# A gated cross-attention and routed feed-forward kernel: mask rows picked in SBUF, one array for the small inputs, another order of constants and first loads

## The chip, the cores and the metric

The kernel runs on 1 core of one Trainium2 chip. The metric is the device time of one execution in microseconds (us), the median of several runs. A profile of one execution shows when each engine worked: TensorE (PE, with its weight loads PEld), VectorE (DVE), ScalarE (ACT), GpSimd (POOL) and SyncE (SP), whose queue issues most of the DMAs.

## The reference

```python
def _L0_xattn_ref(hidden_states, memory_tokens, memory_mask):      # 32 x 112 x 512, 32 x 375 x 512, 32 x 375
    scores = jnp.einsum('bsd,bmd->bsm', hidden_states, memory_tokens) * scale
    scores = jnp.where(memory_mask[:, None, :], scores, neg_inf)
    attn = jax.nn.softmax(scores, axis=-1)
    readout = jnp.einsum('bsm,bmd->bsd', attn, memory_tokens)
    valid_b = jnp.any(memory_mask, axis=-1)
    return jnp.where(valid_b[:, None, None], readout, jnp.zeros_like(readout))

def _L0_ffn_ref(x, Wg, W, b):                                      # Wg 512 x 8, W 8 x 512 x 512
    probs = jax.nn.softmax(jnp.einsum('bsh,he->bse', x, Wg), axis=-1)
    combine = jax.nn.one_hot(jnp.argmax(probs, axis=-1), E) * probs
    y = jnp.einsum('bsh,ehd->bsed', x, W) + b
    return jnp.einsum('bsed,bse->bsd', y, combine)

x = x + jnp.tanh(g_xattn[0]) * _L0_xattn_ref(_layernorm(x), ctx_2048, mask_BxS2_bk0)
x = x + jnp.tanh(g_ffn[0]) * _L0_ffn_ref(_layernorm(x), L0_ffn_Wg, L0_ffn_W, L0_ffn_b)
```

All arithmetic is in 32-bit floats.

## The kernel before

The kernel has two phases. In the first, one batch (112 rows of x, its context of 375 rows) after the other goes through cross-attention and through the choice of one of 8 experts for each row; in the second, tiles of 128 rows, gathered by expert, go through the expert's weights. The change is in the first phase, and mostly ahead of its first batch.

For a batch, TensorE turns the context (four chunks of 128 columns, three transposes each, `ctx_turn`) and the normalised x (`x_turn`, four transposes); ScalarE copies each turned chunk from PSUM (`ctx_part`), VectorE computes the rest that this rounding left (`low_part`); then come the score products (`scores`; eleven, the last of which adds the row of the mask). Softmax follows on VectorE and ScalarE, its weights are turned, and `read_out` multiplies them with the context. Normalisation takes `stats1` on VectorE, a few small steps on POOL (`stats1` there) and `apply1` on ScalarE. The stages of three batches overlap: the iteration `batch(i)` on TensorE scores batch i+1, reads out batch i and turns batch i+2. It runs from i = -2 up; four iterations stand before a loop over four batches a turn. Every engine executes its own list in order and waits on semaphores.

SP's queue issues the loads. There are four buffers for x and context; `load(i+4)` is issued when `x2` of batch i, the rows with attention added, is complete, right after those rows' store to DRAM. `load_w` brings a 128 x 512 part of the expert weights for each batch, which ScalarE and POOL split into two parts (`w_hi`, `w_lo`).

Ahead of the first batch: POOL sets the constants; SP loads the mask, the router weights `wg_sb`, batch 0, the two gate scalars (each spread over 128 partitions), and batch 1; VectorE makes an additive mask of 32 rows, which SP stores to DRAM (`mask_rows`) and loads back one row per batch (`mask_row`, in partition 0 of a cleared tile). TensorE first makes `valid_ps` (which batches have a valid token), waits for `gv_ok` (that, times the gate's tanh), then sums the router weights over their rows in four products (`wg_sum_ps`), from which VectorE subtracts the mean and makes seven copies (`wg_ok`); only then does `batch(-2)` begin:

```python
            pe.wait_ge(wg_ld, 16)
            pe.wait_ge(gv_ok, 1)
            for k in range(KC):
                last = pe.matmul(wg_sum_ps, ones[:, :], wg_sb[:, k, :], start=(k == 0), stop=(k == KC - 1))
            last.then_inc(wg_mm, 1)
            pe.wait_ge(wg_ok, 7)
            for n in range(-2, 0):
                batch(Count(n))
```

Of the kernel before, what the change touches and what calls it, by code (L numbers as in the profile page):

```python
# [27 lines left out]
P = 128  # L28
# [79 lines left out]
def build(nc, x, ctx, mask, g_attn, g_ffn, w_gate, w_exp, b_exp, out):  # L108
    B, S, D = x.shape
    M = ctx.shape[1]  # L110
    E = w_gate.shape[1]
# [25 lines left out]
    FILL = 64  # L137
    assert M == MC * MP and MP <= P and KC * S + E <= 512 and REGION >= N + P and B % TURN == 0 and S < P
# [4 lines left out]
    mask_rows = nc.dram_tensor("mask_rows", (B, M), BF16, kind="Internal").ap()  # L143
    lst = nc.dram_tensor("token_list", (LIST, 4), F32, kind="Internal").ap()

    with ExitStack() as stack:
# [17 lines left out]
        first_only = sb("first_only", [P, P], BF16)  # L164
# [14 lines left out]
        mask_add = late[0:B, D + 128:D + 384].bitcast(BF16)[:, 0:M]  # L179
        wg_sb = sb("wg_sb", [P, KC, E])  # L180
        wg_mid = sb("wg_mid", [P, KC, E])
        mask_row = sb("mask_row", [P, 4, M], BF16)
        any_valid = sb("any_valid", [B, 1])
        any_diag = sb("any_diag", [B, B])
        gate_in = sb("gate_in", [P, 2])
# [81 lines left out]
        valid_ps = small_ps[:, 256:256 + B]  # L267
# [9 lines left out]
        gate_ld, wg_ld, b_ld, mask_ld = sem("gate_ld"), sem("wg_ld"), sem("b_ld"), sem("mask_ld")  # L277
# [4 lines left out]
        mask_in = [sem(f"mask_in{i}") for i in range(4)]  # L282

        fill_st, zero_st, mask_mv = sem("fill_st"), sem("zero_st"), sem("mask_mv")
# [8 lines left out]
        row_clear, first_ok = sem("row_clear"), sem("first_ok")  # L293
# [14 lines left out]
        wg_mm, wg_ok = sem("wg_mm"), sem("wg_ok")  # L308
# [13 lines left out]
        CONSTS = 16  # L322
# [41 lines left out]
        def _(sp):  # L364
# [6 lines left out]
            def load_mask(j):  # L371
                sp.dma_start(mask_row[0:1, j.slot(4), :], mask_rows[bass.ds(j.times(1), 1), :]
                             ).then_inc(mask_in[j.slot(4)], 16)

# [16 lines left out]
            load_w(Count(0))  # L391
            load(Count(2))
            load(Count(3))
            load_w(Count(1))
# [9 lines left out]
            def batch(i):  # L404
# [50 lines left out]
        def _(pool):  # L455
            pool.memset(ident[:, :], 0.0).then_inc(const, 1)
            pool.memset(ones_bf[:, :], 1.0).then_inc(const, 1)
            pool.memset(ones[:, :], 1.0).then_inc(const, 1)
            if ME > M:
# [4 lines left out]
            pool.memset(half[:, :], -0.5).then_inc(const, 1)  # L464
            pool.memset(eps[:, :], EPS).then_inc(const, 1)
            pool.memset(minus[:, :], -1.0).then_inc(const, 1)
            pool.wait_ge(const, 6)
# [835 lines left out]
```

## Time and profile before

| | |
|---|---|
| median of 3 runs | 397.51 us (397.43 to 399.56) |
| profiled execution | 396.76 us, its span 394.9 us |
| TensorE busy | 355.5 us (90%) |
| VectorE, POOL, ScalarE busy | 301.6 (76%), 227.8 (58%), 221.3 us (56%) |
| granted TensorE clock, mean | 0.982 |
| DMA | 67.26 MB, mean 170 GB/s |

The span runs from the first to the last instruction of the profiled execution; the rest of its time lies around it. Busy shares are means over the whole span, and the start, the batches and the tiles have different limits.

### The profile page before, as it was taken

What the parts mean: (1) busy time and instruction counts of PE and PEld (TensorE: products, weight loads), DVE (VectorE), ACT (ScalarE), POOL (GpSimd) and SP (SyncE); (2) the same over time, 40 slices, a digit from 0 to 9 for tenths busy, and PEclk for the clock granted to TensorE, in tenths of its full rate; (3) what the DMA queues carried; (4) which work ended last, traced back from release to release, by engine and by line L of the source; (5) the groups of instructions that cost most, each with busy time, mean ns of one, the idle gap of its engine ahead of it and who ended that gap; (6) DMA issues with size and microseconds to landing.
All of it is one profiled execution on the core that took longest, in us unless ns stands there. A gap on an engine that the chain in (4) does not pass through costs nothing.

```text
span 394.9 us, 9724 instructions
## 1 busy us (share of the span) xinstructions
PE 355.5 (90%) x2012; PEld 299.0 (76%) x2013; DVE 301.6 (76%) x1085; ACT 221.3 (56%) x488; POOL 227.8 (58%) x483
## 2 busy tenths in 40 slices
PE   0889999999999999999999999756999999999980
PEld 0668888788888878888888877635877787878860
DVE  2467989889999889989998889736887677776760
ACT  1267777667777767777776768323444444444410
POOL 6023666566666666666656655565655566666620
PEclk9999999999999999999999999979999999999996
DMA  6586788878889979889888874193445544445410
GB/s 171 146 204 170 185 212 193 194 187 221 201 200 226 188 174 237 191 184 231 209 210 185 202 190 124 42 320 85 125 148 158 162 144 142 132 149 159 152 56 0
DMA packets 40222, 67.26 MB, mean 170 GB/s; under 512 B 11298, under 2 KB 11878, under 8 KB 40200
## 3 DMA queue, kind: packets, MB, share of 16 engines
q1 hardware_dynamic: 33576, 50.43, 52.2%
q0 software_dynamic: 6624, 16.58, 13.3%
q8 instruction: 8, 0.13, 0.2%
q14 instruction: 14, 0.11, 0.1%
HBM read 51.70 MB, written 17.12 MB: 174 GB/s over the span
## 4 chain that ended last, share of the span: by engine, by line
PE 54%; DMA 14%; DVE 10%; issue 8%; POOL 5%; SPq 4%; ACT 2%; POOLq 1%; DVEq 1%; ACTq 0%
PE read_both L1143 8%; PE ctx_ps L1087 8%; PE read_both L1144 7%; DMA ctx_sb<-in_ctx 6%; PE score_ps L1184 4%; PE score_ps L1182 4%; PE score_ps L1183 3%; PE score_ps L1112 3%; POOL out_rows L603 3%; DMA li<-token_list 3%; PE score_ps L1109 3%; PE score_ps L1110 3%; DMA x_sb<-mid_rows,take 3%; PE score_ps L1111 3%; PE prob_ps L1096 2%
## 5 line engine op out<-in xcount | busy, mean ns | idle before, releaser
L1143 PE MATMUL read_both<-ctx_sb 125*112 125x264 f32 x192 | 61.1, 400 | 2.1 <-DVE lg L841 1.8
L1182 PE MATMUL score_ps<-w_hi,ctxT_hi 128*128 x140 | 58.8, 420 | 1.6 <-DVE ctxT_lo L912 1.6
L972 DVE TENSOR_TENSOR ctxT_lo<-ctx_ps,ctxT_hi 128x375 fp32r<-128x375 f32 x96 | 49.5, 542 | 13.9 <-ACT ctxT_hi L641 13.5
L530 POOL DMA_INDIRECT token_list<-pay,pos x32 | 32.6, 1018 | 47.0 <-DVE pos L893 41.5
L1087 PE MATMUL ctx_ps<-ident,ctx_sb 125*128 125x125 f32 x384 | 54.4, 278 | 5.9 <-DMA ctx_sb<-in_ctx 2.6
L1144 PE MATMUL read_both<-ctx_sb 125*112 125x256 f32 x192 | 57.1, 379 | 0.0
L1184 PE MATMUL score_ps<-w_lo,ctxT_hi 128*128 x140 | 55.8, 398 | 0.0
L1183 PE MATMUL score_ps<-w_hi,ctxT_lo 128*128 x140 | 55.4, 396 | 0.0
L1087 PEld LDWEIGHTS ctx_ps<-ident,ctx_sb 125*128 125x128 f32 x384 | 43.8, 145 | 8.4 <-DMA ctx_sb<-in_ctx 3.5
L594 POOL DMA_INDIRECT x_sb<-mid_rows,take x35 | 34.4, 983 | 27.0 <-DVE ctx_sb L930 13.6
L652 ACT ACTIVATE w_raw<-x_sb,li 128x512 f32<-128x512 f32 x35 | 28.5, 815 | 36.9 <-DMA x_sb<-mid_rows,take 36.9
L603 POOL DMA_INDIRECT out_rows<-ctx_sb,put x35 | 39.4, 1126 | 16.9 <-issue 9.2
L641 ACT ACTIVATE ctxT_hi<-ctx_ps 128x375 fp32r<-128x375 f32 x96 | 42.7, 482 | 8.5 <-PE ctx_ps L1087 7.6
L706 ACT ACTIVATE xn<-x_sb,ln 112x512 f32<-112x512 f32 x32 | 26.0, 813 | 30.3 <-POOL ln L494 30.3
L665 ACT ACTIVATE ctxT_hi<-ctx_ps 128x512 fp32r<-128x512 f32 x35 | 20.9, 598 | 36.0 <-PE ctx_ps L1164 36.0
L479 POOL TENSOR_TENSOR w_lo<-w_raw,w_hi 128x512 f32 (+1 forms) x32 | 40.8, 1274 | 0.0
L1144 PEld LDWEIGHTS read_both<-ctx_sb 125*112 125x112 f32 x192 | 34.0, 177 | 8.7
L1109 PE MATMUL score_ps<-ctxT_hi,xnT_hi 128*120 128x384 f32 x96 | 38.0, 396 | 0.9 <-DVE ctxT_lo L972 0.9
L925 DVE SCALAR_TENSOR_TENSOR x_sb<-ctx_sb,li,x_sb 128x512 f32<-128x512 f32 x35 | 26.4, 754 | 13.3 <-issue 12.8
L1143 PEld LDWEIGHTS read_both<-ctx_sb 125*112 125x112 f32 x192 | 29.2, 176 | 5.6 <-issue 2.2
L912 DVE TENSOR_TENSOR ctxT_lo<-ctx_ps,ctxT_hi 128x512 fp32r<-128x512 f32 x35 | 24.2, 691 | 11.6 <-ACT ctxT_hi L665 11.5
L1110 PE MATMUL score_ps<-ctxT_hi,xnT_lo 128*120 128x384 f32 x96 | 32.4, 337 | 0.0
(136 smaller groups left out, 816.0 us busy)
## 6 DMA issues: line engine op xcount, KB each, us to landing
ctx_sb<-in_ctx SPq DMA_DIRECT2D x32, 672.0 KB
w_raw<-in_L_ffn_W SPq DMA_DIRECT2D x32, 256.0 KB, 4.6
x_sb<-in_x SPq DMA_DIRECT2D x32, 224.0 KB, 4.0
mid_rows<-x SPq DMA_DIRECT2D x32, 224.0 KB, 3.1
ctx_sb<-in_ctx SPq DMA_DIRECT2D x32, 78.0 KB
ctx_sb<-in_L_ffn_b SPq DMA_DIRECT2D x8, 256.0 KB, 6.2
li<-token_list SPq DMA_DIRECT2D x35, 2.0 KB, 1.9
x_sb<-mid_rows,take POOLq DMA_INDIRECT x35, 3.4
```

The source lines that it names most:

```text
L479: pool.tensor_tensor(w_lo[:, bass.ds(w.times(D), D)], w_raw[:, w.slot(2), :], w_hi[:, bass.ds(w.times(D), D)].bitcast(F32), ALU.subtract). ...
L603: pool.indirect_dma_start(out, bass.IndirectOffsetOnAxis(put[:, b:b + 1], 0), res[:, b, :], None, bounds_check=N - 1, oob_is_err=False).th ...
L641: act.activation(ctxT_hi[:, k, 0:M], ctx_ps[k % 2][:, 0:M], ACT.Copy).then_inc(ctxT_hi_ok, 1)
L972: dve.tensor_tensor(ctxT_lo[:, k, 0:M], ctx_ps[k % 2][:, 0:M], ctxT_hi[:, k, 0:M].bitcast(F32), ALU.subtract).then_inc(ctxT_ok, 1)
L1087: last = pe.transpose(ctx_ps[k % 2][:, c * MP:(c + 1) * MP], ctx_sb[0:MP, MC * j.slot(4) + c, SE + k * P:SE + (k + 1) * P], ident[0:MP, 0:MP])
L1109: pe.matmul(score_ps[a][0:SE, 0:MG], xnT_hi[:, k, :], ctxT_hi[:, k, :], start=(k == 0), stop=False)
L1110: pe.matmul(score_ps[a][0:SE, 0:MG], xnT_lo[:, k, :], ctxT_hi[:, k, :], start=False, stop=False)
L1143: pe.matmul(read_a, turned[:, 0:S], turned[:, S:SE + HALF], start=(c == 0), stop=(c == MC - 1))
L1144: last = pe.matmul(read_b, turned[:, 0:S], turned[:, SE + HALF:], start=(c == 0), stop=(c == MC - 1))
L1182: pe.matmul(y_ps[a][:, :], hi, w_hi[:, chunk], start=(k == 0), stop=False)
L1183: pe.matmul(y_ps[a][:, :], lo, w_hi[:, chunk], start=False, stop=False)
L1184: last = pe.matmul(y_ps[a][:, :], hi, w_lo[:, chunk], start=False, stop=(k == KC - 1))
```

## The change

Mask rows: the additive mask stays in SBUF as `mask_add` (128 partitions, rows 32 and up zero). The last score product takes as its weights column j of the identity, repeated with step 0, so that row j is picked; store, loads and `mask_row` go away. Small inputs: the host lays router weights and both scalars in one array of 128 x 34, which ScalarE's queue loads, as it does the mask. Router sum: VectorE adds the four parts first, and one product is left. Constants: POOL sets those of the start first, the others (`router_constants`) after the first statistics. TensorE: 40 and 16 products of constants ahead of `batch(-2)`, and the wait for `wg_ok` now ahead of the first scores. `x_turn` of batch 0 goes ahead of chunks 2 and 3, and chunks 0 and 1 of context 1 go behind the scores of batch 0. SP waits for `st1_ok` ahead of load 1, for `xnT_ok` ahead of load 2 and for context 1 ahead of the second part of the weights.

```diff
@@ build
+    WARM, WARM_MORE = 40, 16
-        valid_ps = small_ps[:, 256:256 + B]
+        valid_ps = read_both[:, 0:B]
+        warm_ps = score_ps[1][:, 0:P]
...
@@ sync
-            sp.dma_start(mask_u8[:, :], mask).then_inc(mask_ld, 16)
-            sp.dma_start(wg_sb[:, :, :], w_gate.rearrange("(k p) e -> p k e", p=P)).then_inc(wg_ld, 16)
             load(Count(0))
-            sp.dma_start(gate_in[:, 0:1], g_attn.rearrange("(a b) -> a b", a=1).to_broadcast([P, 1])).then_inc(gate_ld, 16)
-            sp.dma_start(gate_in[:, 1:2], g_ffn.rearrange("(a b) -> a b", a=1).to_broadcast([P, 1])).then_inc(gate_ld, 16)
+            sp.wait_ge(st1_ok, 1)
             load(Count(1))
-            sp.wait_ge(mask_ok, 2)
-            sp.dma_start(mask_rows, mask_add[:, :]).then_inc(mask_mv, 16)
-            sp.wait_ge(mask_mv, 16)
-            sp.wait_ge(row_clear, 1)
-            for j in range(4):
-                load_mask(Count(j))
             load_w(Count(0))
+            sp.wait_ge(xnT_ok, 1)
             load(Count(2))
+            sp.wait_ge(ctx_ld[1], 32)
+            load_w(Count(1))
             load(Count(3))
-            load_w(Count(1))
...
                     load(i.plus(4))
-                    load_mask(i.plus(4))
@@ gpsimd
-            pool.memset(ident[:, :], 0.0).then_inc(const, 1)
             pool.memset(ones_bf[:, :], 1.0).then_inc(const, 1)
+            pool.memset(ident[:, :], 0.0).then_inc(ident_ok, 1)
+            pool.memset(mask_add[:, :], 0.0).then_inc(mask_clear, 1)
...
-            pool.memset(mask_row[:, :, :], 0.0).then_inc(row_clear, 1)
...
                 if at == -3:
-                    late_constants()
+                    router_constants()
@@ scalar
-            act.wait_ge(gate_ld, 32)
+            act.dma_start(mask_u8[:, :], mask).then_inc(mask_ld, 16)
+            act.dma_start(small_sb[:, :], small).then_inc(small_ld, 16)
+            act.wait_ge(small_ld, 16)
             act.activation(gate_th[:, :], gate_in[:, :], ACT.Tanh).then_inc(th_ok, 1)
...
+                    if at == -1:
+                        weights(ahead)
+                        act.wait_ge(w_ld[0], 16)
                     act.activation(w_hi[:, bass.ds(ahead.times(D), D)], w_raw[:, ahead.slot(2), :], ACT.Copy
                                    ).then_inc(w_hi_ok, 1)
-                    if at != B - 2:
+                    if at not in (-1, B - 2):
                         weights(ahead)
@@ vector
+            def sum_router():
+
+                dve.wait_ge(small_ld, 16)
+                dve.tensor_reduce(wg_part[:, :], wg_sb[:, :, :].rearrange("p k e -> p e k"), AX.X, ALU.add).then_inc(wg_part_ok, 1)
+
+            def mark_valid():
+                dve.wait_ge(ident_ok, 2)
+                dve.tensor_copy(ident_bf[:, :], ident[:, :]).then_inc(select_ok, 1)
+                dve.wait_ge(mask_ok, 2)
+                dve.tensor_scalar(any_diag[:, :], ident[0:B, 0:B], any_valid[:, :], None, ALU.mult).then_inc(any_ok, 1)
...
                 if at == -3:
+                    sum_router()
+                    mark_valid()
+                    center_router()
                     which_valid()
-                    center_router()
@@ tensor
-                pe.wait_ge(mask_in[j.slot(4)], j.rounds(4) * 16 + 16)
-                pe.matmul(score_ps[a][0:S, 0:M], first_only[:, 0:S], mask_row[:, j.slot(4), :],
+                pe.matmul(score_ps[a][0:S, 0:M], ident_bf[:, bass.ds(j.times(1), 1)].to_broadcast([P, S]), mask_add[:, :],
                           start=False, stop=True).then_inc(score_mm, 1)
...
                 if at == -1:
-
-                    ctx_turn(turned, 0)
-                    ctx_turn(turned, 1)
+                    pe.wait_ge(select_ok, 1)
+                    pe.wait_ge(mask_ok, 2)
+                    pe.wait_ge(wg_ok, 7)
...
-            pe.wait_ge(any_ok, 1)
-            pe.matmul(valid_ps, ones[0:B, :], any_diag[:, :], start=True, stop=True).then_inc(valid_mm, 1)
-            pe.wait_ge(wg_ld, 16)
-            pe.wait_ge(gv_ok, 1)
-            for k in range(KC):
-                last = pe.matmul(wg_sum_ps, ones[:, :], wg_sb[:, k, :], start=(k == 0), stop=(k == KC - 1))
-            last.then_inc(wg_mm, 1)
-            pe.wait_ge(wg_ok, 7)
...
+            pe.wait_ge(const, 1)
+            for n in range(WARM):
+                pe.matmul(warm_ps, ones_bf[:, :], ones_bf[:, :], start=True, stop=True)
+            router_sum()
+            valid_sum()
+            for n in range(WARM_MORE):
+                pe.matmul(warm_ps, ones_bf[:, :], ones_bf[:, :], start=True, stop=True)
+            pe.wait_ge(ident_ok, 2)
             for n in range(-2, 0):
                 batch(Count(n))
```

On TensorE the program began with these rows, from the valid sum (L1259) and the router sum (L1263) to the first score product of batch 0 (L1109); `ctx_ps` holds the turned context and `prob_ps` the turned x.

```order
L1259 MATMUL small_ps<-any_diag,w_lo 128x32
L1263 MATMUL small_ps<-wg_sb,w_lo 128x8 x4
L1087 MATMUL ctx_ps<-ident,ctx_sb 128x125 x12
L1096 MATMUL prob_ps<-ident,xn 128x112 x4
L1087 MATMUL ctx_ps<-ident,ctx_sb 128x125 x6
L1109 MATMUL score_ps<-ctxT_hi,xnT_hi 120x384
```

With the change the same place on TensorE reads as follows, where L1260 and L1264 are the products of constants and L1082 the transposes of the context.

```order
L1260 MATMUL score_ps<-ones_bf 128x128 x40
L1252 MATMUL small_ps<-wg_part,w_lo 128x8
L1256 MATMUL read_both<-any_diag,w_lo 128x32
L1264 MATMUL score_ps<-ones_bf 128x128 x16
L1082 MATMUL ctx_ps<-ident,ctx_sb 128x125 x6
L1091 MATMUL prob_ps<-ident,xn 128x112 x4
L1082 MATMUL ctx_ps<-ident,ctx_sb 128x125 x6
L1104 MATMUL score_ps<-ctxT_hi,xnT_hi 120x384
```

The router sum has one product and stands between the two groups of constants, x is turned in the middle of context 0, and context 1 is no longer turned ahead of the first scores.

On SP's queue the first twelve DMAs were these (L366 is a load of x, L368 and L369 of its context).

```order
L379 DMA w_lo<-in_mask_BxS_bk 32x375
L380 DMA wg_sb<-in_L_ffn_Wg 128x4x8
L366 DMA x_sb<-in_x 112x512
L368 DMA ctx_sb<-in_ctx 112x3x512
L369 DMA ctx_sb<-in_ctx 13x3x512
L382 DMA gate_in<-in_g_xattn 128x1
L383 DMA gate_in<-in_g_ffn 128x1
L366 DMA x_sb<-in_x 112x512
L368 DMA ctx_sb<-in_ctx 112x3x512
L369 DMA ctx_sb<-in_ctx 13x3x512
L386 DMA mask_rows<-w_lo 32x375
L372 DMA mask_row<-mask_rows 1x375 x4
```

With the change SP's queue begins with the first two loads and the first part of the weights (L373), then the third load and the second part.

```order
L366 DMA x_sb<-in_x 112x512
L368 DMA ctx_sb<-in_ctx 112x3x512
L369 DMA ctx_sb<-in_ctx 13x3x512
L366 DMA x_sb<-in_x 112x512
L368 DMA ctx_sb<-in_ctx 112x3x512
L369 DMA ctx_sb<-in_ctx 13x3x512
L373 DMA w_raw<-in_L_ffn_W 128x512
L366 DMA x_sb<-in_x 112x512
L368 DMA ctx_sb<-in_ctx 112x3x512
L369 DMA ctx_sb<-in_ctx 13x3x512
L373 DMA w_raw<-in_L_ffn_W 128x512
```

Mask, router weights and scalars have left the queue, and load 0 stands first.

## Rows read from the trace of the kernel before

**Rows 1.** The page's span in 40 slices: TensorE busy, granted clock, in tenths.

```profile
PE   0889999999999999999999999756999999999980
PEclk9999999999999999999999999979999999999996
```

**Rows 2.** Timeline of TensorE at the start: start, us, operation, count, idle before and releaser.

```profile
10.24 1.85 PE L1263 MATMUL small_ps<-wg_sb,w_lo 128*128 128x8 f32 x8 [3.84 <-DVE gv L797]
13.13 1.51 PE L1087 MATMUL ctx_ps<-ident,ctx_sb 125*128 125x125 f32 x6 [1.05 <-DVE ctxT_full L814]
...
18.74 0.40 PE L1109 MATMUL score_ps<-ctxT_hi,xnT_hi 128*120 128x384 f32 x1
...
21.02 0.32 PE L1114 MATMUL score_ps<-mask_row,first_only 128*112 128x375 bf16 x1
...
22.56 0.99 PE L1087 MATMUL ctx_ps<-ident,ctx_sb 125*128 125x125 f32 x6 [0.83 <-DVE ctxT_lo L972]
24.45 0.41 PE L1109 MATMUL score_ps<-ctxT_hi,xnT_hi 128*120 128x384 f32 x1 [0.90 <-DVE ctxT_lo L972]
...
27.22 0.81 PE L1087 MATMUL ctx_ps<-ident,ctx_sb 125*128 125x125 f32 x6
28.24 0.70 PE L1143 MATMUL read_both<-ctx_sb 125*112 125x264 f32 x2 [0.21 <-ACT ctx_sb L691]
```

**Rows 3.** Timeline of SP's queue at the start.

```profile
0.79 0.40 SPq L379 DMA_DIRECT2D w_lo<-in_mask_BxS_bk  x1
...
1.71 0.49 SPq L366 DMA_DIRECT2D x_sb<-in_x  x1
...
5.04 0.43 SPq L366 DMA_DIRECT2D x_sb<-in_x  x1
...
14.84 0.43 SPq L366 DMA_DIRECT2D x_sb<-in_x  x1
```

**Rows 4.** Timeline of POOL, VectorE and ScalarE at the start.

```profile
0.93 0.21 POOL L457 MEMSET ones_bf<- 128x128 bf16 x1
...
4.60 0.69 DVE L779 BATCH_NORM_STATS2 st<-x_sb 112x6 f32<-112x512 f32 x1 [1.24 <-DMA x_sb<-in_x]
...
6.61 0.19 POOL L494 TENSOR_TENSOR ln<-ve,ln 112x1 f32<-112x1 f32 x1
...
9.53 0.20 ACT L633 ACTIVATE gate_th<-gate_in 128x2 f32<-128x2 f32 x1 [7.46 <-DMA gate_in<-in_g_ffn]
9.64 0.80 ACT L706 ACTIVATE xn<-x_sb,ln 112x512 f32<-112x512 f32 x1
```

**Rows 5.** DMA view of 0 to 20 us: GB/s per half microsecond; an issue's landing.

```profile
GB/s 0 0 0 23 15 52 143 279 127 131 328 385 238 267 136 148 242 336 315 287 258 241 101 28 15 3 0 0 3 2 34 61 324 414 176 82 233 328 369 250
...
w_lo<-in_mask_BxS_bk SPq DMA_DIRECT2D x1, 11.7 KB, 1.6
```

**Rows 6.** The page's costliest groups: busy us, mean ns of one, idle before.

```profile
L972 DVE TENSOR_TENSOR ctxT_lo<-ctx_ps,ctxT_hi 128x375 fp32r<-128x375 f32 x96 | 49.5, 542 | 13.9 <-ACT ctxT_hi L641 13.5
...
L641 ACT ACTIVATE ctxT_hi<-ctx_ps 128x375 fp32r<-128x375 f32 x96 | 42.7, 482 | 8.5 <-PE ctx_ps L1087 7.6
```

**Rows 7.** Timeline of SP's queue in the loop: stores of finished rows, batches 0, 1, 26.

```profile
33.17 0.35 SPq L409 DMA_DIRECT2D mid_rows<-x  x1
...
40.33 0.33 SPq L409 DMA_DIRECT2D mid_rows<-x  x1
...
224.30 0.33 SPq L409 DMA_DIRECT2D mid_rows<-x  x1
```

**Rows 8.** The tile of the mask row: count, ns min/median/max, first and last start.

```profile
L372 SPq DMA_DIRECT2D mask_row<-mask_rows x32: 232/247/414, 13.3 to 235.4; - x32
L1114 PEld LDWEIGHTS score_ps<-mask_row,first_only x32: 128/130/130, 20.7 to 249.4; 128*112 128x112 bf16 x32
```

**Rows 9.** Waits (us, times, longest us): SP's queue to 60 us; TensorE, whole span.

```profile
SPq L409 <- DVE x L828: 14.3, 4, 4.5
...
PE ctx_ps L1087 <- DMA ctx_sb<-in_ctx: 2.6, 4, 0.8
```

More of the change, by code:

```diff
@@ L105, in run, with build @@
         body(Count(n))
-def build(nc, x, ctx, mask, g_attn, g_ffn, w_gate, w_exp, b_exp, out):
+def build(nc, x, ctx, mask, small, w_exp, b_exp, out):
     B, S, D = x.shape
     M = ctx.shape[1]
-    E = w_gate.shape[1]
+    E = b_exp.shape[0]
     N = B * S
@@ L462, in _ @@
                 pool.memset(ctxT_full[:, M:ME], 0.0).then_inc(pad_ok, 1)
-            pool.memset(mask_row[:, :, :], 0.0).then_inc(row_clear, 1)
[L464 to L467, printed above, removed]
-            pool.affine_select(out=ident[:, :], in_=ident[:, :], compare_op=ALU.not_equal, fill=1.0, base=0,
-                               pattern=[[-1, P]], channel_multiplier=1).then_inc(const, 1)
-            pool.affine_select(out=first_only[:, :], in_=ones_bf[:, :], compare_op=ALU.is_ge, fill=0.0, base=0,
-                               pattern=[[0, P]], channel_multiplier=-1).then_inc(first_ok, 1)
+            pool.memset(unused[:, :, :], 0.0).then_inc(fill_ok, 1)
+            pool.wait_ge(fill_ok, 1)
+            pool.memset(unused[:, :, 0:1], float(NO_TOKEN)).then_inc(fill_ok, 1)
+            pool.wait_ge(const, 5)
             filing = Stage(pool, "filing", -2)
@@ L531, in file @@
                                         pay[:, j.slot(4), :], None).then_inc(list_st[j.slot(4)], 16)
-            pool.iota(token_ids[:, :], [[S, B]], base=0, channel_multiplier=1).then_inc(const, 1)
-            pool.memset(zeros[:, :], 0.0).then_inc(zero_ok, 1)
-            pool.affine_select(out=before[:, :], in_=ones_bf[:, :], compare_op=ALU.is_gt, fill=0.0, base=0,
-                               pattern=[[1, P]], channel_multiplier=-1).then_inc(const, 1)
-            pool.iota(rev[:, :], [[-1, E]], base=E, channel_multiplier=0,
-                      allow_small_or_imprecise_dtypes=True).then_inc(const, 1)
@@ L736, in batch @@
                 if soon.within(B):
-                    if at != -2:
-                        turned_x(soon)
+                    turned_x(soon)
                     ctx_part(soon, 2)
-                if ahead.within(B):
+                if ahead.within(B) and at != -1:
                     act.wait_ge(w_ld[ahead.slot(2)], ahead.rounds(2) * 16 + 16)
@@ L1033, in batch @@
                     place(gated)
-                if soon.within(B) and at != -2:
+                if soon.within(B):
                     turned_x(soon)
-                if soon.within(B):
                     low_part(soon, 2)
@@ L1128, in ranks @@
                 a = j.slot(2)
+                if j.turn is None and j.at == 0:
+                    pe.wait_ge(const, 9)
                 pe.wait_ge(hot_ok, j.times(1, 1))
@@ L1140, in read_out @@
                         pe.wait_ge(lg_ok, j.times(1))
+                    else:
+                        pe.wait_ge(gv_ok, 1)
                 turned = ctx_sb[0:MP, MC * j.slot(4) + c, :]
@@ L1218, in batch @@
                     turn_weights(now)
-                if turned.within(B) and at != -1:
+                if turned.within(B):
                     ctx_turn(turned, 0)
@@ L1291 @@
     arrays, args = {}, []
+    gate_rows = _np.asarray(inputs["L0_ffn_Wg"])
+    gate_rows = gate_rows.reshape(-1, 128, gate_rows.shape[1]).transpose(1, 0, 2).reshape(128, -1)
+    scalars = [_np.broadcast_to(_np.asarray(inputs[n]).reshape(1, 1), (128, 1)) for n in ("g_xattn", "g_ffn")]
+    inputs = dict(inputs, small=_np.concatenate([gate_rows] + scalars, axis=1))
     for name in _INS:
```

108 lines of the change are left out of this document (52 added, 56 removed).

## The prediction

> **What bounds the kernel now.** The page comes first: in 40 slices TensorE is busy for nine tenths or more nearly everywhere; the first slice (9.9 us) is empty, the next two are at 8, and some near the middle and the end are lower [rows 1]. The change works on the start. TensorE's timeline there [rows 2] shows the router sum at 10.24, the first transpose of context 0 at 13.13, the first score product of batch 0 at 18.74, that of batch 1 at 24.45, and the first read-out product at 28.24. From the fourth slice on TensorE is full.
>
> What holds the 13.13? The rows of the other engines [rows 4] give the chain backwards: transposes behind the last router copy on VectorE (the releaser in the row of 13.13), those copies behind the router sum on TensorE (10.24, 1.85 us), that behind gv on VectorE (its releaser), that behind the tanh on ScalarE at 9.53, which had sat idle for 7.46 us for the two gate scalars. These stand on SP's queue behind x 0 and context 0. The layer norm of batch 0 was ready far earlier (its last POOL step at 6.61), but stands behind the tanh on ScalarE (9.64).
>
> Context 0 was not what was waited for. In the flow of bytes [rows 5] the slices of 0.5 us sum to 994 kB at 7.0 us and 1062 kB at 7.5; by their shapes mask (12 kB), router weights (16), x 0 (229) and context 0 (768) are 1025 kB, so if the queue serves in order context 0 was in at about 7.2 us. Some 6 us lie between that and the first transpose.
>
> After the start a batch takes 7.16 us at first (SP stores x2 at 33.17 and 40.33), and 7.35 on the mean up to 224.30 (26 batches) [rows 7]. Each batch's stored rows release the load four batches on, so the loop runs by its own distances: a start that is earlier by so much should move everything behind it by as much.
>
> **The change, part by part.** The profiled execution took 396.76 us (span 394.9, 1.86 around it); the median shown is 397.51, 0.75 more. Removed work in the loop first: the mask row's load, 0.25 us of SP's issuing per batch [rows 8]. No row waits for it, and SP itself waits for x2 (14.3 us in four waits at the start [rows 9]). I price it at 0. Bounds: 0, and 32 times 0.25 = 8 us of gain if SP's queue were the bound, which its waits exclude. The product that adds the mask has the same size; only its weights now come from one column of the identity with step 0. The nearest weight load is 0.13 us [rows 8], under a longer fp32 product: 0 again, with a rival below.
>
> Start of the transposes, T0. Two things must be there.
> - Context 0. x 0 goes out at 0.79, SP's first slot, in place of 1.71 [rows 3], so everything of context 0 moves 0.92 earlier: 6.3 us. Mask and gates now go on ScalarE's queue at that time; the mask landed 1.6 us after its issue [rows 5], the other array (17 kB) is as small, and their cover is the 3 us before x 0 is in. If they are mixed with context 0 instead, it costs a few tenths.
> - TensorE. The 40 + 16 products of 128 columns begin when ones_bf is set, now POOL's first instruction: 0.79 + 0.21 [rows 3, 4] = 1.0. Six transposes of 125 columns (fp32, two passes) take 1.51 us at 13.13 and 0.81 at 27.22 [rows 2], one pass about 0.105 or 0.053 us; so 40 bf16 products take 2.2 to 4.3 us and end at 3.2 to 5.3. The router sum waits for VectorE: x 0 in at 0.79 + 2.89 = 3.68 (issue 1.71, bn_stats at 4.60 [rows 3, 4]), bn_stats 0.69, two small steps of 0.2: 4.8 us. One product instead of four (1.85 / 4 = 0.46), then the valid sum, as much again, held until the identity's copy and any_diag are done (two more small steps, 5.4): 5.9. Then 16 more products, 0.9 to 1.7: TensorE is free at 6.9 to 8.1. I take 7.1, nearer the lower end since products of that row's pace were reached once TensorE had worked for 5.6 us.
>
> So T0 = 7.1 against 13.13: **-6.0 us**. The router copies now run beside the transposes (wg_ok is asked for only by the first scores): sum at about 5.5, seven small VectorE steps as between 12.09, the end of the sum before, and 13.13: done at about 6.6. Their cover is the whole transposing stage; without it they cost 1 us. x 0 normalised: the last POOL step ended at 6.80, 2.20 after bn_stats began, plus 0.8 of ScalarE [rows 4]: 3.68 + 3.0 = 6.7, before its transposes. POOL's constants that went behind it (router_constants) run while POOL has nothing else until the statistics of batch 1.
>
> T0 to the first scores took 5.6 us. With the clock up and x's transposes ahead of chunks 2 and 3 the chain is three transposes 0.5, ScalarE's copy 0.48, VectorE's rest 0.54, then transposes of chunk 2, copy and rest once more, and a hop of 0.05 at each step [rows 2, 6]: 3.4 us. ScalarE's copy of x (smaller than one of a chunk) fits before that of chunk 2. Scores at 10.5: **-2.2 us**.
>
> First scores to second took 5.71 (18.74 to 24.45). Chunks 0 and 1 of context 1, formerly turned before the scores, now come behind them: 2.65 us of scores (18.74 to 21.34, and a hop) and another 3.4 = 6.05: **+0.35 us**. Second scores at 16.55. Are context 1 and 2 there? SP issues load 1 when bn_stats of x 0 is done, 4.4 against 5.04, so it is in by about 10.7 (the bytes of the first two loads were through by 11.5 [rows 5]; needed at 13.2). Load 2 waits for xnT_ok, about 9.6, against 14.84 [rows 3], weights 0 ahead of it; behind what is still in the queue its 1 MB is in at about 15.5, and wanted at 19.4. What is queued behind that wait (weights 1, load 3, the list's fill) has some 7 us to spare.
>
> Second scores to the first read-out (3.79) keeps its chain; x 2's statistics now stand behind the softmax bias: **+0.1 us**. First read-out at 20.4 to 20.5 in place of 28.24.
>
> Sum: -6.0 - 2.2 + 0.35 + 0.1 = -7.75; 396.76 - 7.75 = 389.0, and 0.75 more on the scale of the median: **389.7 us**.
>
> **Clock.** The granted clock reads full (2.4 GHz) over the start [rows 1], yet the transposes of batch 0, to 18.7 us, run at near half the pace of those at 27.22 [rows 2]; after the first score products they were at full pace, and a stretch of transposes alone (six in 0.99 us at 22.56, a wait of 0.83 before the row) did not lose it. By the durations then the early products raise the pace and the 3.4 us of transposes keep it. The Trainium skill speaks against this ("TensorE: Matmul & The Clock Gate", Part 4: PE-mode transpose): transposes do not count as work that brings the full clock. The slow transposes of batch 0 agree with it; those at 27.22, amid other products, run fast all the same.
>
> **The rivals.**
> - The pace falls back. If T0 to the scores is transposes only and TensorE drops to the slow level, the stage keeps most of its 5.6 us and the first scores (2.6 us) run slow for about half their length: 1.8 + 1.2 us back, 392.7. For it: the slow transposes at 13.13 to 18.7 although TensorE was busy. Against: the six at 22.56. The rule just cited would act so, by this mechanism.
> - The DMA queue takes the gain back. In the loop 26 batches lost 0.19 us each against 7.16, 5 us [rows 7], and TensorE waited for contexts four times, 2.6 us [rows 9]; if the queue is the true bound, only idle time removed from it counts: the hole of 11.5 to 15.5 us [rows 5] and 0.9 at the start, some 4.9 us of gain: 392.6. For it: those losses. Against: loads are released by finished batches, so a delay is not made up by a queue that stood idle early.
> - Each load on its own: context 2 or 3 is late since it waits for xnT_ok. It needs more than 3.9 us of delay over the 15.5; each us beyond costs one. 391 to 392.
> - Slower: the weight load from one column with step 0 has no row. If each took so long that a batch's score group grew by more than 7.75 / 32 = 0.24 us, the change loses: at 0.35 the time is 401. Against: 0.13 us for the same 112 columns, with a longer product in front to hide it.
> - It does nothing: excluded unless the start is not on the path; that TensorE is full from the fourth slice on speaks against it.
>
> **How the numbers follow.** My forecast (388.0 to 391.2 by T0 from 6.4 to 8.1 and the spread of runs) has 0.58; pace 0.13; queue 0.15; late loads 0.07; slower 0.04; none or next to none 0.03. Leaving 0.1 at each end gives 386.8 to 393.2. A measurement tells 0.5%, 2 us, from no change: faster 0.92, same 0.04, slower 0.04.
>
> **What would show it.** Right: first transpose near 7, scores near 10.5 and 16.5, first read-out near 20.5, six transposes in about 0.8 us, and x2 stores that begin near 25.4 with the same spacing. Wrong: a tanh or router sum that again ends after 6 us, a first transpose behind the 16 products beyond 8 us, transposes at 1.5 us for six, TensorE waiting for a context between 12 and 30 us, or a batch longer than 7.35 on the mean.

## The result and the profile after

The changed kernel took 393.17 us (median of 4 runs, 392.07 to 394.58); the kernel before, over 4 runs, 398.53 (397.43 to 402.15): a ratio of 0.9886 (95% interval 0.9846 to 0.9926), some 4.5 us. The ratios, here and below, are of the fast runs alone and need not be the quotients of the medians beside them. Forecast were 389.7 us and a gain of 7.75. Beside the later runs, with 17 to 28 runs of the kernel before each, the same kernel gave 0.9899 (0.9863 to 0.9934) and 0.9894 (0.9859 to 0.9930). The profiled execution of the change took 394.58 us, its span 392.8.

The page's slices first (TensorE busy, granted clock, in tenths; beside [rows 1]; the clock of the first slices is no reading, as shown below), then TensorE's timeline at the start (start, us, operation; beside [rows 2]):

```profile
PE   7799999999999999999999999376999999999980
...
PEclk9999999999999999999999999968999999999995
```

```profile
1.06 4.45 PE L1260 MATMUL score_ps<-ones_bf 128*128 128x128 bf16 x40 [1.06 <-POOL ones_bf L444]
5.52 0.43 PE L1252 MATMUL small_ps<-wg_part,w_lo 128*128 128x8 f32 x2
...
6.22 1.07 PE L1264 MATMUL score_ps<-ones_bf 128*128 128x128 bf16 x16
8.18 0.83 PE L1082 MATMUL ctx_ps<-ident,ctx_sb 125*128 125x125 f32 x6 [0.89 <-DMA ctx_sb<-in_ctx]
...
11.74 0.40 PE L1104 MATMUL score_ps<-ctxT_hi,xnT_hi 128*120 128x384 f32 x1 [0.90 <-DVE ctxT_lo L968]
...
17.72 0.40 PE L1104 MATMUL score_ps<-ctxT_hi,xnT_hi 128*120 128x384 f32 x1 [0.90 <-DVE ctxT_lo L968]
...
21.57 0.70 PE L1141 MATMUL read_both<-ctx_sb 125*112 125x264 f32 x2 [0.28 <-ACT ctx_sb L680]
```

First transposes 8.18 against 13.13, first scores 11.74 against 18.74, read-out 21.57 against 28.24: the start is 6.67 us shorter. TensorE was through with its products at 7.29 (6.22 + 1.07) and then waited 0.89 for context 0. The engines ahead of it (beside [rows 4]), SP's first loads of x (beside [rows 3]) and its stores in the loop (beside [rows 7]):

```profile
0.79 0.20 POOL L444 MEMSET ones_bf<- 128x128 bf16 x1 [0.29 <-POOLq L1288]
...
3.49 0.53 DVE L758 TENSOR_SCALAR mask_add<-w_lo 32x375 bf16<-32x375 uint8 x1 [3.37 <-DMA w_lo<-in_mask_BxS_bk]
...
4.40 0.67 DVE L769 BATCH_NORM_STATS2 st<-x_sb 112x6 f32<-112x512 f32 x1
...
3.84 0.20 ACT L622 ACTIVATE gate_th<-small_sb 128x2 f32<-128x2 f32 x1 [0.82 <-DMA small_sb<-in_small]
```

```profile
0.79 0.40 SPq L366 DMA_DIRECT2D x_sb<-in_x  x1
...
5.10 0.36 SPq L366 DMA_DIRECT2D x_sb<-in_x  x1
...
10.69 0.33 SPq L366 DMA_DIRECT2D x_sb<-in_x  x1
...
26.38 0.35 SPq L398 DMA_DIRECT2D mid_rows<-x  x1
33.55 0.34 SPq L398 DMA_DIRECT2D mid_rows<-x  x1
...
216.88 0.34 SPq L398 DMA_DIRECT2D mid_rows<-x  x1
```

26 batches took 190.50 us here and 191.13 before: the loop passed the start on, 6.79 us at the first store and 7.42 at the 27th. What is lost is lost behind the loop. There the second phase begins with POOL's gather of the first tile's rows, which ScalarE then normalises (timelines of POOL and ScalarE, the kernel before and then the change):

```profile
254.92 1.00 POOL L594 DMA_INDIRECT x_sb<-mid_rows,take  x1 [0.16 <-issue]
...
260.22 0.81 ACT L652 ACTIVATE w_raw<-x_sb,li 128x512 f32<-128x512 f32 x1 [4.15 <-DMA x_sb<-mid_rows,take]
```

```profile
247.51 1.00 POOL L581 DMA_INDIRECT x_sb<-mid_rows,take  x1 [0.16 <-issue]
...
254.84 0.81 ACT L641 ACTIVATE w_raw<-x_sb,li 128x512 f32<-128x512 f32 x1 [6.46 <-DMA x_sb<-mid_rows,take]
```

The gather is issued 7.41 us earlier, its rows are used 5.38 earlier: it took 5.30 us before and takes 7.33 now. TensorE stands in this wait (waits: us, times, longest; beside [rows 9]):

```profile
PE ctx_ps L1162 <- ACT w_raw L641: 10.6, 7, 5.5
PE ctx_ps L1082 <- DMA ctx_sb<-in_ctx: 2.6, 4, 0.9
```

The waits for contexts are what they were. Before, the first of these rows read 7.1 us, 5 times, 3.2 at most.

### The profile page after: what moved, and what is told of

Read it like the earlier page. It is cut to its first block, busy times and chain, and to the rows that moved or that the text cites. A ratio compares the mean times of both kernels' runs of the same rounds, so it can differ in the third digit from the quotient of the medians.

```text
span 392.8 us, 9753 instructions
## 1 busy us (share of the span) xinstructions
PE 359.2 (91%) x2062; PEld 302.1 (77%) x2063; DVE 301.0 (77%) x1087; ACT 220.6 (56%) x488; POOL 226.8 (58%) x482
## 4 chain that ended last, share of the span: by engine, by line
PE 52%; DMA 16%; issue 9%; DVE 7%; POOL 6%; ACT 3%; SPq 3%; POOLq 1%; DVEq 1%; ACTq 0%
DMA ctx_sb<-in_ctx 8%; PE read_both L1141 8%; PE ctx_ps L1082 8%; PE read_both L1142 7%; DMA x_sb<-mid_rows,take 6%; PE score_ps L1180 4%; PE score_ps L1107 3%; POOL out_rows L590 3%; PE score_ps L1182 3%; PE score_ps L1181 3%; PE score_ps L1104 3%; PE score_ps L1105 3%; PE score_ps L1106 3%; PE prob_ps L1091 2%; PE ctx_ps L1162 2%
## 5 line engine op out<-in xcount | busy, mean ns | idle before, releaser
L1180 PE MATMUL score_ps<-w_hi,ctxT_hi 128*128 x140 | 59.7, 426 | 1.6 <-DVE ctxT_lo L908 1.6
L1082 PE MATMUL ctx_ps<-ident,ctx_sb 125*128 125x125 f32 x384 | 52.6, 272 | 4.4 <-DMA ctx_sb<-in_ctx 2.6
L1181 PE MATMUL score_ps<-w_hi,ctxT_lo 128*128 x140 | 56.3, 402 | 0.0
L1082 PEld LDWEIGHTS ctx_ps<-ident,ctx_sb 125*128 125x128 f32 x384 | 42.4, 141 | 7.0 <-DMA ctx_sb<-in_ctx 2.7
L926 DVE SCALAR_TENSOR_TENSOR ctx_sb<-score_ps,li,x_sb 128x512 f32<-128x512 f32 x35 | 26.3, 751 | 8.7 <-PE score_ps L1182 7.7
## 6 DMA issues: line engine op xcount, KB each, us to landing
w_raw<-in_L_ffn_W SPq DMA_DIRECT2D x32, 256.0 KB, 5.1
ctx_sb<-in_L_ffn_b SPq DMA_DIRECT2D x8, 256.0 KB, 7.6
```

The lines of the kernel that those rows point to most:

```text
L1082: last = pe.transpose(ctx_ps[k % 2][:, c * MP:(c + 1) * MP], ctx_sb[0:MP, MC * j.slot(4) + c, SE + k * P:SE + (k + 1) * P], ident[0:MP, 0:MP])
L1180: pe.matmul(y_ps[a][:, :], hi, w_hi[:, chunk], start=(k == 0), stop=False)
L1181: pe.matmul(y_ps[a][:, :], lo, w_hi[:, chunk], start=False, stop=False)
```

## The experiments

Times from "issue of the first gather to ScalarE's first normalised rows" are called the first gather below.

**Is the gain stable, and what are the products worth?** e1 is the change unaltered. e2 leaves out the 56 products that only occupy TensorE:

```diff
-    WARM, WARM_MORE = 40, 16
+    WARM, WARM_MORE = 0, 0
```

e3 holds load 1 back until context 0 is in:

```diff
             sp.wait_ge(st1_ok, 1)
+            sp.wait_ge(ctx_ld[0], 32)
             load(Count(1))
```

> The changed kernel unaltered, to see what of its time repeats. Theory A (the gain of the start passes on in full, and the tile phase of the profiled execution was a bad draw): stores of the last finished rows again near 252.6 us, and a tile phase after that store of about 135 us as before the change, so a span near 388 and a ratio near 0.980 to 0.984. Rival B (the tile phase is longer with the change): again some 140 us behind the last store, span near 392, ratio near 0.989.

> The 56 products of constants ahead of the first transposes are left out (their result is used nowhere). Theory A (they set the pace of the first transposes): first transpose again near 8.2 us since context 0 is waited for, six transposes in about 1.5 us in place of 0.83, first scores 1.3 to 2 us later than 11.74, first read-out near 23 to 23.5 in place of 21.57, the total 1.5 to 2 us longer. Rival B (the pace is not theirs to set, or hidden): first scores within 0.3 us of 11.74 and no difference in total.

> SP issues load 1 only when all of context 0 is in, in place of after the first statistics. Theory A (context 0 lands at 8.0 us because load 1, issued from 5.1, shares the DMA engines with it): first transpose at 6.8 to 7.2 in place of 8.18, that is what I had forecast; context 1 comes later, at 12 to 13, still in time for 14.2, so a first read-out near 20.5. Rival B (context 0 is late through its own slowest engine): first transpose at 8.0 to 8.3 still, load 1 issued at 8.1, and context 1 either just in time or waited for up to 1 us at 14.3.

Measured beside one another, 28 runs of the kernel before at 399.57 us: e1 395.78, ratio 0.9899 (0.9863 to 0.9934); e2 396.82, 0.9940 (0.9903 to 0.9978); e3 396.40, 0.9924 (0.9887 to 0.9961). TensorE's timeline in e1:

```profile
6.60 1.89 PE L1264 MATMUL score_ps<-ones_bf 128*128 128x128 bf16 x16
8.28 1.46 PE L1082 MATMUL ctx_ps<-ident,ctx_sb 125*128 125x125 f32 x6
...
12.33 0.41 PE L1104 MATMUL score_ps<-ctxT_hi,xnT_hi 128*120 128x384 f32 x1 [0.89 <-DVE ctxT_lo L968]
```

With the same 56 products as in the first profile, the 16 took 1.89 us, not 1.07, and the six transposes 1.46, not 0.83: full pace came only by the scores, 0.6 us lost. Behind its last store e1 took 139.6 us, the change's first profile 140.1: the second phase did not come out shorter. Without the products (e2) the scores too ran slow, and the read-out began at 24.02: against e1's 22.17 the products are worth 1.85 us at that place. In time e2 lies 1.0 us above e1, with intervals that overlap. In e3 the transposes began at 7.40, but context 1 then was late by 1.68 us and the read-out began at 22.69: nothing gained.

**Pacing.** e7 takes SP's three waits between its first loads out:

```diff
-            sp.wait_ge(st1_ok, 1)
             load(Count(1))
             load_w(Count(0))
-            sp.wait_ge(xnT_ok, 1)
             load(Count(2))
-            sp.wait_ge(ctx_ld[1], 32)
             load_w(Count(1))
             load(Count(3))
```

> The change with SP's three waits between its first loads taken out: load 1, weights 0, load 2, weights 1 and load 3 are issued back to back behind load 0. Theory A (loads that stand on the queue at once share the DMA engines, as load 1 did with context 0 in e3, where context 0 landed 0.8 us earlier once load 1 was held): context 0 lands at 9 to 10.5 us in place of 8.0 to 8.2, the first read-out is later by 1 to 2.5 us, and the time is 0.5 to 2.5 us above the change's. Rival (the queue serves in order, pacing is worth nothing): first transposes at 8.0 to 8.4 and the same time within 0.5 us. A third, that x 0 itself is late by sharing: bn_stats later than 5.5 us and a router sum behind it.

394.82 us, ratio 0.9907 (0.9857 to 0.9958), as the change. The transposes began at 7.59, no later. So the pacing by compute has no part that these runs can tell, and e3's earlier context 0 isn't shown to come from load 1: over the profiles of the change and its variants that leave the first loads alone, T0 lay between 7.59 and 8.85.

**The first gather and the bias loads.** Right with that gather SP issues eight loads that spread the experts' bias rows over 128 partitions (256 KB each). e4 moves them behind the landing of the first two gathers, e6 does the same to the kernel before, e5 is the kernel before unaltered:

```diff
-            sp.wait_ge(read_mm, B - 3)
-            for e in range(0, MC):
-                load_bias(e)
...
             batch(Count(B - 1))
+            sp.wait_ge(read_mm, B - 1)
+            sp.wait_ge(row_ld[0], 16)
+            sp.wait_ge(row_ld[1], 16)
+            for e in range(0, E):
+                load_bias(e)
```

> SP loads the eight expert bias rows (256 KB each, spread over the partitions) only when the first two gathers of rows have landed; it formerly issued six of them at the time of the first gather. Theory A (the first gather of the tile phase takes 7.3 us because it shares the DMA engines with the bias loads, and TensorE then waits 5.5 us and runs the next products at half pace): the first gather lands in 3 to 4 us, TensorE's wait ahead of the first tile falls to 1 to 3 us, the total falls by 2 to 4 us. Rival B (the gather is late for itself, or the biases are then what is late): the gather still takes 5 us and more, or VectorE waits for the biases at its first tile; the total is the same or 1 to 3 us longer.

> The kernel before, unaltered, for a second profile. The stretch from the last x2 store to the end took 135.2 us in its first profile and 139.5 to 140.2 in two profiles of the change. Theory A (the tile phase varies from run to run and the first profile of before was a good draw): this profile has 137 to 140 us there, a profiled time of 398.5 to 401, with the first read-out product again near 28.2. Rival (the change itself lengthens the tile phase, for instance since its first gather meets the bias loads differently): 135 to 136 us again and a time near 397. A third: the start of before is what varies; then its first read-out is more than 0.5 us off 28.2.

> The kernel before with only the eight bias loads moved behind the landing of the first two gathers (the same edit as in e4, without the change). Theory A (the meeting of bias loads and first gather is in both kernels and the change has no part in it): the first gather takes about 4.1 us to ScalarE's first normalised rows in place of 5.3 to 7.3, and the time falls by 1 to 3 us, a ratio of 0.993 to 0.9975 to before. Rival (only the change brings them together, so e4 repaired something that the change had done): ratio 0.999 to 1.001.

e4: 393.85 us, 0.9839 (0.9795 to 0.9882), some 0.6% below e1 with intervals that overlap a little, and a first gather of 4.1 us. e6: 400.90 us, 1.0124 (1.0030 to 1.0217), outside both ranges that were expected; against the median of all 23 runs of the kernel before beside it, 399.81, it is 0.3% more, so a loss isn't certain, but the gain of e4 is missing. That points to something which the change has and the kernel before hasn't. e5 took 400.67 us, with 5.73 us for the first gather, and 140.4 us behind the last store where the first profile had 135.3 and the change's 140.1: that profile of before, on which the sum was made, was a good draw in the second phase. The longer draw goes with a second fall of the clock: in the second phase the trace's clock records read 0.50 from 261.32 to 268.14 and from 274.97 to 281.80 us in e5, and only from 260.95 to 267.78 in the first profile. No run tests that by itself.

What the change has shows in the DMA view of 2 us, from 1 us behind the gather's issue: the second profile of before (254.9 to 256.9) and the change (248.5 to 250.5).

```profile
DMA packets 229, 0.44 MB, mean 219 GB/s; under 512 B 21, under 2 KB 21, under 8 KB 229
```

```profile
DMA packets 50, 0.10 MB, mean 51 GB/s; under 512 B 0, under 2 KB 0, under 8 KB 50
```

The bias loads' first packets stall: 50 of them kept the DMA engines busy for 92% of the 2 us. By the trace's packet records those of 2 KB that began in 248.5 to 249.0 took 1.33 us each (median); in the first profile of before, in 256.0 to 256.5, 0.09. The gathers' packets come behind them.

Four kernels ask what in the change does it. f1 declares the bias array first, which should shift the arrays' places in the chip's memory (no trace here shows addresses); f2 adds an unused tile that should put x_sb, ctx_sb and what follows back to their old places in SBUF; f3 brings the scratch array mask_rows back and writes it once; f4 also its 32 loads:

```diff
-_INS = ["x", "ctx_2048", "mask_BxS2_bk0", "small", "L0_ffn_W", "L0_ffn_b"]
+_INS = ["L0_ffn_b", "x", "ctx_2048", "mask_BxS2_bk0", "small", "L0_ffn_W"]
...
-    build(nc, *args, out)
+    build(nc, *args[1:], args[0], out)
```

```diff
+        pad = sb("pad", [P, 1109], BF16)
         x_sb = sb("x_sb", [P, 4, D])
```

```diff
+    mask_rows = nc.dram_tensor("mask_rows", (B, M), BF16, kind="Internal").ap()
...
+            sp.wait_ge(mask_ok, 2)
+            sp.dma_start(mask_rows, mask_add[0:B, :]).then_inc(mask_mv, 16)
+            sp.wait_ge(mask_mv, 16)
+            for j in range(4):
+                load_mask(Count(j))
...
                     load(i.plus(4))
+                    load_mask(i.plus(4))
```

> The change with the bias array declared first among the input arrays, not last (all else alike). In all five profiles of the change whose bias loads stand where they stood, the first gathered rows reach ScalarE 7.3 to 7.4 us behind the gather's issue, in the two of before 5.3 and 5.7; in the second 2 us of the bias loads the DMA engines moved 44 packets (e1) against 230 (before, second profile). Theory A (where the arrays lie in the chip's memory changed, since the change takes away and joins arrays, and the bias rows' reads now meet something there): here the stretch is another one, 5.2 to 6 us, and the bias packets flow from the start. Rival B (not the place of the bias array; its loads meet another part of the change): 7.2 to 7.5 us again.

> The change with an unused tile of 2218 bytes a partition ahead of x_sb, so that x_sb, ctx_sb and all behind them lie where they lay before in SBUF. Theory C (where ctx_sb lies in SBUF decides how the broadcast bias rows are taken): 5.2 to 6 us from the first gather's issue to ScalarE's normalised rows. Rivals A and B (memory arrays, or another part): 7.2 to 7.5 us again.

> The change with the scratch array mask_rows back between mid_rows and token_list, written once behind SP's first loads and never read. Theory A (the places of arrays in memory, here of token_list behind mask_rows): 5.2 to 6 us for the first gather. Rival (it was the loads of mask rows, or the input arrays): 7.2 to 7.5 us.

> The change with the mask rows' store and its 32 loads back on SP's queue, into a tile that nothing reads (the score product keeps the row picked in SBUF). Theory D (the loads, a row of 750 bytes each batch on SP's queue, had been keeping something ready or set the queue's order): 5.2 to 6 us for the first gather, and SP's issue some 0.25 us longer in a batch. Rival (the place in memory alone, or an input's): as in the run with the store alone. The time itself: SP's issue is hidden, so within 1 us of the change's, 393 to 396, unless the first gather changes.

Packets in the same stretch of 2 us and the first gather: f2 57 packets, 7.25 us; f3 50, 6.97; f4 15, 7.32. And f1 (247.2 to 249.2), 5.37 us:

```profile
DMA packets 250, 0.49 MB, mean 243 GB/s; under 512 B 24, under 2 KB 24, under 8 KB 250
```

Only the order of the arrays takes the stall away. Single times here were 390.66, 390.89, 393.92 and 393.95 us in the order f1 to f4, too spread to rank (f2 has the stall and is low).

**Is the stall the missing time, and what stands behind it?** All on one chip: g1 the change, g2 the bias array first, g3 that and TensorE kept busy in the wait for the first rows, g4 the kernel before with the bias array first. e8 had tried the fillers (32 and 24) with the late bias loads of e4. The edit of g3:

```diff
+            def fill(n):
+                for _ in range(n):
+                    pe.matmul(warm_ps, ones_bf[:, :], ones_bf[:, :], start=True, stop=True)
...
                 if at == B - 1:
+                    fill(56)
                     tile(Count(-1))
+                    fill(24)
```

> The change, with the bias loads behind the first two gathers as in e4, and TensorE filled where it waits for the first gathered rows: 32 products of 128 columns before the transposes of tile 0 and 24 between them and its products (their results are not used). Theory A (TensorE drops to the lower of its levels in that wait and then runs the first dozen products of the tile phase at half pace; kept busy it stays at full pace): six to twelve products of tile 0 at 0.39 us each and 0.23 apart, not 0.63 and 0.43, the time 1.5 to 3 us below that of e4, 391 to 392.5 on the scale of 397.5 before. Rival (the pace falls by TensorE's own history before the wait, not by the wait): the clock still reads 0.5 for 4 to 8 us there and the time is that of e4 within 0.5 us, or above it by what the fillers outlast the gather, up to 1.5 us.

> The change, unaltered, timed beside the next three on the same chip. By the two runs so far: a ratio of 0.988 to 0.991 to before; first gathered rows 7.3 to 7.4 us behind the gather's issue.

> The change with the bias array declared first, now timed. Theory A (the slow first packets of the bias loads, a matter of where the array lies, cost the change 1.6 to 2 us at the first gather, on the path): 1.5 to 2.5 us below the change on the same chip, a ratio to before of 0.983 to 0.986. Rival (what is lost there has slack, the list loads or the last two batches' routing set the start of the tile phase): within 0.5 us of the change.

> The bias array first, and TensorE filled with 56 products of 128 columns ahead of the transposes of tile 0 and 24 behind them (results unused). Theory (TensorE drops to half pace in the wait for the first gathered rows): products of tile 0 at 0.39 us and not 0.63, a further 1 to 2 us below the run with the bias array first alone, a ratio of 0.978 to 0.983. Rival (the time is held by the gathers and lists there, not by TensorE's pace): as the run before within 0.5 us; and if the fillers outlast the gather, up to 1 us above it.

> The kernel before with the bias array declared first. Its bias packets flowed from the start already (first gather 5.3 and 5.7 us), so by theory A nothing is to be had: ratio 0.997 to 1.003. Rival (the order of arrays helps by something else that both kernels have, such as the loads of contexts or weights): 0.99 to 0.996, and then a part of what the run with the bias array first shows is not the stall.

| kernel | median us | ratio to before (95% interval) | first gather us |
|---|---|---|---|
| before, 17 runs | 400.20 | 1 | 5.3, 5.7 |
| g1 the change | 395.64 | 0.9894 (0.9859 to 0.9930) | 7.6 |
| g2 bias array first | 393.72 | 0.9834 (0.9792 to 0.9876) | 5.4 |
| g3 and fillers | 390.52 | 0.9728 (0.9693 to 0.9764) | 6.2 |
| g4 before, bias array first | 401.47 | 1.0027 (1.0002 to 1.0051) | 5.8 |

The order of arrays is worth 1.9 us to the change and nothing to the kernel before. The intervals of g1 and g2 overlap, but the first gather agrees in every profile: 7.0 to 7.6 us in the nine with the change's order of arrays and early bias loads, 5.3 to 5.8 in the three of the kernel before (g4 among them) and 5.4 in f1 and g2; g3's 6.2 has no stall at its start. TensorE's waits agree too. Its longest for ScalarE's normalised rows, 5.5 us in the change, was 5.1 to 5.7 in those nine, 3.2 to 3.9 in those three and 3.5 and 3.6 in f1 and g2; the row of g2 reads:

```profile
PE ctx_ps L1162 <- ACT w_raw L641: 6.8, 6, 3.6
```

So the stall is on the path, and it's the change's own. The fillers gave 3.2 us more, where 1 to 2 were expected. TensorE's timeline of tile 0's products in the change, then in g3:

```profile
255.70 1.11 PE L1162 MATMUL ctx_ps<-ident,w_raw 128*128 128x128 f32 x4 [5.49 <-ACT w_raw L641]
258.39 0.79 PE L1180 MATMUL score_ps<-w_hi,ctxT_hi 128*128 x1 [1.57 <-DVE ctxT_lo L908]
258.98 0.63 PE L1181 MATMUL score_ps<-w_hi,ctxT_lo 128*128 x1
```

```profile
256.41 0.66 PE L1162 MATMUL ctx_ps<-ident,w_raw 128*128 128x128 f32 x4 [1.24 <-ACT w_raw L641]
...
258.66 0.50 PE L1180 MATMUL score_ps<-w_hi,ctxT_hi 128*128 x1 [0.25 <-DVE ctxT_lo L908]
259.00 0.39 PE L1181 MATMUL score_ps<-w_hi,ctxT_lo 128*128 x1
```

And the granted clock there (windows: sum, PE busy, clock, DMA share, GB/s) in g1, then g3:

```profile
256.00:260.00 4.00, 1.19 (x5) 0.50 1.05 399
260.00:264.00 4.00, 4.00 (x11) 0.50 0.44 117
```

```profile
256.00:260.00 4.00, 3.33 (x34) 1.00 1.05 402
260.00:264.00 4.00, 3.02 (x19) 1.00 0.33 95
```

Left idle for 5 us TensorE is granted the lower level (1.2 GHz, 0.50) and works through tile 0 at half pace; kept busy it stays at 2.4.

e8 came to 392.66 us, 0.9867 (0.9823 to 0.9911), no lower than e4's 0.9839, where 1.5 to 3 us less had been expected: the products ran at 0.39 us there too, but VectorE then waited for a list:

```profile
263.49 0.15 DVE L891 CAST take<-li 128x1 uint32<-128x1 f32 x1 [4.96 <-DMA li<-token_list]
```

The lists of the next tiles stand on SP's queue behind the eight bias loads, so loads moved late there come back as a late list: VectorE's wait at that place was 3.49 us in e4 and 2.69 in e6, and at most 1.25 in g2 and g3. In e6 this can eat what its shorter first gather (4.84 us) gives, and in e4 and e8 a part of it; another order of arrays has no such price. g3 is the best kernel of this study, faster than both.

## Why the prediction was wrong

The steps, in its order:

- **T0, 13.13 to 7.1, -6.0 us: mis-sized.** It is -4.95 (8.18). TensorE's side was nearly as worked out, free at 7.29, though by another way: the mask landed 2.7 us after its issue, not 1.6, its two VectorE steps stood in front of bn_stats (4.40, not 3.68), and the router sum came at 5.52 for 4.8. (The bounds of 6.9 to 8.1 don't follow from their terms: 5.9 and 0.9 to 1.7 make 6.8 to 7.6.) What failed is the price of context 0. "If the queue serves in order context 0 was in at about 7.2 us", less 0.92, gave 6.3. The trace's records of landings have its last part in at 9.02 us before and at 8.04 with the change: the shift is as forecast, 0.98, but the 7.2 was 1.8 us too early. The sum of bytes moved is no landing time. With load 1 issued at once (e7) context 0 was in at 7.45 and with load 1 held back (e3) at 7.27, so sharing with load 1 isn't shown to be what was missed.
- **T0 to scores, 5.6 to 3.4:** 3.56. **To the second scores, 6.05:** 5.98. **To the read-out, 3.89:** 3.85. These three terms held. The read-out came at 21.57, 1.1 us later than forecast, nearly all of it from T0.
- **Loop and mask at 0:** right. The product that adds the mask takes 0.322 us as before, and the weight load from one column with step 0 costs what the old one did:

```profile
L1108 PE MATMUL score_ps<-mask_add,ident_bf x30: 322/322/323, 20.0 to 233.7; 128*112 128x375 bf16 x30
L1108 PEld LDWEIGHTS score_ps<-mask_add,ident_bf x29: 128/130/130, 27.2 to 233.4; 128*112 x24, 128*112 128x112 bf16 x5
```

  Its rival of a loss has nothing behind it.
- **"A start that is earlier by so much should move everything behind it by as much": the step that failed.** It held through the loop and not at the first gather, where 2.0 us went (7.33 for 5.30). Nothing in the change's code touches that place; it changes which arrays lie in memory, and with their order changed once more the loss is gone (f1, g2). The prediction took the removed arrays for removed transfers alone and had no term for what they do to the second phase; by g1 and g2 that term is 1.9 us.
- **The scale.** 396.76 us, the profile that the sum was made against, and the median of 397.51 lie low: three later sets of 17 to 28 runs had medians of 399.57 to 400.20, and its second profile took 400.67. In the ratio this drops out. That 393.17 lies inside the range of 386.8 to 393.2, at its very end, is luck of the same kind: two later sets of the change had medians of 395.78 and 395.64.
- **Clock.** "The granted clock reads full (2.4 GHz) over the start" is no reading. In the trace of the kernel before the clock records begin at 18.61 us, and the page counts a stretch without a record as full, its mean of 0.982 too. The pace rose where the records begin: at 18.61 before, 5.67 in the change, 10.21 in e1, 16.07 in e2. Ahead of that TensorE worked at the lower level's pace: in e2 a score product took 0.52 us from 13.02 to 15.26, where nothing is recorded, in g2 0.53 in a stretch recorded at 0.50, and at full pace it takes 0.34. So clock and durations don't contradict each other there.

Put together: -6.67 at the read-out and +2.03 at the gather make -4.6, from one profile of each kernel; the three ratios of the change make -4.0 to -4.5 us of 397.51.

The rivals. "The DMA queue takes the gain back" named 392.6, near the measured time, but not by its mechanism: the loop lost nothing (190.50 against 191.13 us for 26 batches), and contexts were waited for as before, 2.6 us, so a late load ("each load on its own") isn't seen either. "The pace falls back" is real: of the 13 profiles of kernels with the 56 products three show the granted clock at 0.50 near T0, here e4 (windows; its clock records read 0.50 from 10.70 to 17.52 us):

```profile
8.00:10.00 2.00, 1.17 (x10) 1.00 1.02 275
10.00:12.00 2.00, 1.41 (x7) 0.67 0.88 172
12.00:14.00 2.00, 1.41 (x5) 0.50 0.77 199
...
16.00:18.00 2.00, 2.00 (x10) 0.62 1.01 244
```

The read-out then began at 24.74 (e4), 24.80 (g2) and 22.73 (g1, a shorter fall), against 21.57 in the change's profile: 3.2, 3.2 and 1.2 us, some 0.6 on the mean over the 13. In two more, e1 and e8, full pace came late (records from 10.21 and 9.76 us). The Trainium skill's rule that was weighed ("TensorE: Matmul & The Clock Gate", Part 4: PE-mode transpose), that transposes don't count as work that brings the full clock, agrees with e4 and with the slow transposes of e2; in the change's own profile the same transposes stayed at full pace from 8.18 on. The rule tells what can happen there, not how often.

What stays open: by which property of a place the first bias packets stall, and whether it's the bias array's own place or that of another that shifts with it. The place in SBUF (f2), the scratch array (f3) and its loads (f4) are excluded.

## What to carry to other kernels

A shorter start passes through a loop that runs by its own distances, but only as far as the next place where a phase begins: look there, at the first gather and at what is issued with it, before the gain is booked. Joining or dropping arrays may move the others in memory; where one row is read by many packets at once, try another order of declarations and compare packets in a stretch of 2 us. Where TensorE must wait some microseconds for a first transfer, products whose results nobody uses were worth more (3.2 us) than taking away part of the wait (1.9). A stretch of the clock row that has no record behind it tells nothing: compare the durations of equal products.

## What the runs showed of the hardware

The first packets of a broadcast load, 128 reads of one row of 2 KB, ran at 219 to 243 GB/s in the kernel before and in the change with the bias array declared first, and at 15 to 77 for 2 us in the change with its own order of arrays; the place in SBUF and the scratch array made no difference. The Trainium skill ("DMA: Bandwidth & Descriptors", Latency and other measured facts) gives 0.2 us for an access to HBM on the average and 2 us at high load; the median of 1.33 us a packet stood here in a stretch of 51 GB/s, so the bytes that this core moved are not its cause.

The same 56 products at the same time of the start brought TensorE to full pace before 6.2 us in one execution and only behind 10 us in another (16 of them in 1.07 and in 1.89 us), and the trace's clock records begin at 5.67 and at 10.21 us. Two profiles of the kernel before, 396.76 and 400.67 us, lay 3.9 us apart, nearly the change's whole gain: one profile of a kernel doesn't give its time.

In every profile but g3's the granted clock fell to 0.50 in the wait for the first gathered rows or right behind it; in e8, which filled that wait too, it fell a little later, in the wait for the list.
